# Small heads' outputs computed with the values stationary, on four 32-column strips, and transposed back

## The chip, the cores and the metric

One Trainium2 chip, one of its cores. The metric is the device time of one execution in microseconds (us). TensorE is called PE here, VectorE DVE, ScalarE ACT, GpSimd POOL, SyncE SP.

## What is computed

Thirty-two sequences of 128 tokens with 128 features pass through four blocks. All data is float32.

- L0: a transformer decoder layer (self attention, cross attention, feed forward; 16 heads of 64), on the whole path of each group.
- L1: attention with 16 heads of 8 features. With `q = relu(x Wq + bq)`, `k`, `v` alike, it is `softmax(q k' / sqrt(8)) v + x`.
- L2: an encoder and decoder layer with linear attention.
- L3: layer norms, attention with 8 heads of 16 features, then a linear recurrence over the 128 tokens and a projection.

The change touches one product in L1 and L3, the softmax weights times the values:

```
attn = jax.nn.softmax(score, axis=-1)
a = jnp.einsum('bhqk,bhkd->bhqd', attn, vh)      # d = 8 (L1) or 16 (L3)
```

The kernel leaves the weights unnormalised (exp(score - max)), carries a column of ones beside each head's values, so that one product gives both the sum over the values and the sum of the weights, and divides afterwards.

## The kernel before

The sequences are worked on in 8 groups of 4 (`G = 4`). There are two streams of work, written as generators and interleaved step by step in the same way on every engine. The **main** stream computes L0 of group g, in the order of the table `MAIN_ORDER` (160 steps). The **side** stream computes L1, L2 and L3 of group g-1, in 85 steps; `SIDE_AT` (L84) says before the end of which main step each side step is taken. So there is a first pass with main alone, seven passes with both (pass 1 to pass 7 below), and then group 8's L1 to L3 with nothing of L0 left: there `last(i)` runs beside `ahead(i)`, the part that does not wait for it. The recurrence and the output end the program. Every engine executes its own list strictly in order and waits on semaphores; so an instruction that waits holds everything behind it on its engine.

The small attentions are `attention_small` (side) and `attention_last` (last group). The unit of work is four heads of one sequence: 4 units per sequence in L1 (`per = 4`), 2 in L3 (`per = 2`), and two units make a pair: 8 pairs in L1, 4 in L3, 12 per pass. A pair's steps:

1. `scores` (L942, in the last group L1128): two products, 512 columns each, into banks 5 and 6 of PSUM.
2. DVE takes the maxima (`maxes`, L1688), ACT the exponentials (`exps`, L1441, 8 instructions of 128 columns in the side stream, the `s_probs` rows).
3. PE transposes the weights, 8 transposes of 128x128 (L969, last: L1135), ACT and DVE copy them to `s_probsT`.
4. `outputs` (L955, last: L1149): per head one product with the transposed weights (128x128) as the stationary operand and the head's values as the moving one, which has 9 columns in L1 and 17 in L3. It is issued behind the scores of the next pair. The result has the tokens on the partitions:

```
for h in range(4):
    at = (q * 4 + h) * d1
    last = mm(bank(SIDE, (tag, "o", b))[:, at:at + d1], s_probsT[:, n, h * 128:h * 128 + 128],
              value[:, b, q * 4 + h, :], start=True, stop=True)
```

5. Once per sequence DVE divides (`divide`, L1809 and L1811; in L1 also an addition, L1816) straight out of bank 7.

A float32 product appears in the trace as two LDWEIGHTS (PEld) and two MATMUL records, so 8 products are "x16"; a transpose is one record of each. Of the main stream these lines are spoken of: L810 (projections, 512 columns), L858 (scores of the large heads, 64 rows of the array each), L868 (transposes), L882 (outputs of the large heads, two heads side by side on two halves of the array's columns), L854 (masks), the ACT copies at L1435 and the exponentials in `probs`. `keep_busy` (L800) issues bf16 products whose result nobody reads.

The arrays of the streams' fills (`side_fills`, `last_fills`) list which bank each item is put in and which engine empties it; the counts that semaphores are waited for come from them.

Of the kernel before, what the change touches and what calls it, by code (L numbers as in the profile page):

```python
# [31 lines left out]
G = 4  # L32
# [27 lines left out]
def main_items(name):  # L60
# [11 lines left out]
    if name == "mk":  # L72
# [70 lines left out]
def side_fills():  # L143
# [3 lines left out]
    def attention(tag):  # L147
        per = SMALL[tag][0] // 2
        for j in range(PAIRS[tag] + 1):
            if j < PAIRS[tag]:  # L150
                order.extend(((tag, "s", 2 * j + n), 5 + n, "A") for n in range(2))
            if j and j % per == 0:
                order.append(((tag, "o", j // per - 1), 7, "D"))
            if j < PAIRS[tag]:
                order.extend(((tag, "t", 2 * j + n), 5 + n, "AD"[n]) for n in range(2))

# [30 lines left out]
def last_fills():  # L187
# [8 lines left out]
    def attention(tag):  # L196
# [8 lines left out]
        for j in range(pairs):  # L205
            order.extend(((tag, "t", 2 * j + n), (5, 6, 0, 1)[2 * (j % 2) + n], "AD"[n]) for n in range(2))
            scalar.extend([(tag, "s", 2 * j + 2)] if j + 1 < pairs else [])
            scalar.append((tag, "t", 2 * j))
            scalar.extend([(tag, "s", 2 * j + 3)] if j + 1 < pairs else [])
            if j and j % per == 0:  # L210
                order.append(((tag, "o", j // per - 1), 7, "D"))
            if j + 2 < pairs:
                scores(j + 2)
        order.append(((tag, "o", G - 1), 7, "D"))
# [105 lines left out]
def build_program(nc, I, out):  # L320
    with ExitStack() as ctx:
# [76 lines left out]
        l1v = sb("l1v", [128, G, H1, D1 + 1])  # L398
        l2v = sb("l2v", [128, G, 129])
        l3v = sb("l3v", [128, G, H3, D3 + 1])  # L400
# [40 lines left out]
        l3b_last = queries[:, 1, :]  # L441
        x2_all = sb("x2_all", [128, T, B])
# [144 lines left out]
        def _(pool):  # L587
# [28 lines left out]

            link(P.memset(l1v[:, :, :, D1:D1 + 1], 1.0))
# [31 lines left out]
            def side(i):  # L649
# [17 lines left out]
                for _ in range(3 * PAIRS["l1"] + 1):  # L667
# [33 lines left out]
                for _ in range(3 * PAIRS["l3"] + 1):  # L701
# [10 lines left out]
            def last(i):  # L712
# [9 lines left out]
                for _ in range(2 * PAIRS["l1"] + 2):  # L722
# [29 lines left out]
                for _ in range(2 * PAIRS["l3"] + 2):  # L752
# [37 lines left out]
        def _(pe):  # L790
# [139 lines left out]
            def attention_small(i, tag, value):  # L930
# [14 lines left out]
                def outputs(j):  # L945
                    b = 2 * j // per
                    for n in range(2):
# [12 lines left out]
                for j in range(PAIRS[tag]):  # L960
# [5 lines left out]
                    for n in range(2):  # L966
# [18 lines left out]
            def side(i):  # L985
# [12 lines left out]
                yield from attention_small(i, "l1", l1v)  # L998
# [71 lines left out]
                yield from attention_small(i, "l3", l3v)  # L1070
# [47 lines left out]
            def attention_last(i, tag, value, spread_keys):  # L1118
# [20 lines left out]
                def outputs(j):  # L1139
                    b = 2 * j // per  # L1140
                    for n in range(2):
# [3 lines left out]
                        if q == 0:  # L1145
                            hold(i, LAST, (tag, "o", b))
                        for h in range(4):
                            at = (q * 4 + h) * d1
                            last = mm(bank(LAST, (tag, "o", b))[:, at:at + d1],  # L1149
                                      last_probsT[j % 2][:, n, h * 128:h * 128 + 128],  # L1150
                                      value[:, b, q * 4 + h, :], start=True, stop=True)
# [6 lines left out]
                for j in range(PAIRS[tag]):  # L1158
                    keep_busy(4, 4)
                    turns(j)  # L1160
                    yield
                    keep_busy(0, 4)
# [4 lines left out]
                    yield  # L1167
                outputs(PAIRS[tag] - 1)
                yield
# [969 lines left out]
```

## Time and profile before

| what | value |
|---|---|
| median of 3 runs | 2230.75 us (2226.66 to 2233.94) |
| the profiled execution's own time | 2236.29 us |
| its span, first to last instruction | 2234.6 us |
| mean granted clock of TensorE | 0.961 of 2.4 GHz |
| PE busy | 1989.1 us, 89% |
| DVE, ACT, POOL busy | 60%, 49%, 11% |
| chain that ended last | PE 59%, DVE 21%, ACT 15%, issue 4% |

The profile's page gives busy shares, the chain of work that ended last (followed back from the last instruction, at each step to what released it) and groups of instructions. The timeline, the chain in order of time, and windows (busy time and granted clock of a stretch) come from the trace of the same execution. The granted clock is a share of full speed: 0.50 is the lower of its two levels, 1.2 GHz, and 1.00 the upper, 2.4 GHz.

### The profile page before, as it was taken

To read this page: it belongs to the slowest core of one execution; us is meant where nothing else is said; L and a number is where in the kernel's file an instruction comes from. 1 tells how busy PE (TensorE), PEld (TensorE's weight loads), DVE (VectorE), ACT (ScalarE), POOL (GpSimd) and SP (SyncE) were. 2 spreads that over 40 slices of the span, in tenths; PEclk is the share of its full clock that TensorE was granted. 3 is DMA by queue.
4 is the path that set the end of the run, shared out by engine and by line. 5 is a ranking of instruction groups with operands and counts; after the bars stand their busy time and mean duration, and the time that the engine had idled before them with its cause. 6 is when DMAs were issued, how large, how long until landed. Compare 5 with 4: busy or idle time off the path is not lost.

```text
span 2234.6 us, 35672 instructions
## 1 busy us (share of the span) xinstructions
PE 1989.1 (89%) x13350; PEld 1347.7 (60%) x13457; DVE 1332.3 (60%) x3612; ACT 1093.0 (49%) x3794; POOL 238.2 (11%) x261
## 2 busy tenths in 40 slices
PE   6877998899889998899889998899889998888799
PEld 3555665657656665656656675656656675656455
DVE  4443667566675667566675667666675657654410
ACT  4452745557362735546363645547363745533222
POOL 0001011010112011010111001010212001010100
PEclk9998999999999999999999999999999999998999
DMA  6000000000000000000000000000000000000001
GB/s 186 1 1 16 1 1 1 1 16 1 1 1 16 1 1 1 1 16 1 1 1 16 1 1 1 1 16 1 1 1 5 1 1 1 1 1 1 1 11 28
DMA packets 25137, 20.13 MB, mean 9 GB/s; under 512 B 2243, under 2 KB 22790, under 8 KB 24966
## 3 DMA queue, kind: packets, MB, share of 16 engines
q1 hardware_dynamic: 24966, 17.83, 2.8%
q8 instruction: 109, 1.79, 0.3%
q14 instruction: 62, 0.51, 0.1%
HBM read 15.73 MB, written 2.10 MB: 8 GB/s over the span
## 4 chain that ended last, share of the span: by engine, by line
PE 59%; DVE 21%; ACT 15%; issue 4%; POOL 1%; SPq 1%; DMA 0%; POOLq 0%; DVEq 0%; ACTq 0%
PE ps L810 13%; PE ps L818 10%; ACT probs L1441 7%; PE ps L858 6%; PE ps L955 5%; ACT s_probs L1441 4%; PE ps L882 3%; DVE neg_max L1688 3%; PE ps L969 3%; PE ps L806 3%; PE ps L800 2%; PE ps L868 2%; PE ps L942 2%; PE ps L854 2%; PE ps L1389 2%
## 5 line engine op out<-in xcount | busy, mean ns | idle before, releaser
L1441 ACT ACTIVATE probs<-ps,neg_max 128x128 f32<-128x128 f32 x1024 | 360.3, 378 | 248.2 <-DVE neg_max L1688 247.2
L1688 DVE TENSOR_REDUCE neg_max<-ps 128x4 f32<-128x512 f32 x256 | 164.6, 685 | 126.7 <-PE ps L858 126.6
L1441 ACT ACTIVATION_READ_ACCUMULATOR probs<-ps,neg_max 128x1 f32 x1024 | 221.8, 217 | 0.0
L632 POOL TENSOR_TENSOR rstd<-var_eps,minus_half 128x4 f32<-128x4 f32 x88 | 94.4, 1073 | 1125.9 <-DVE var_eps L1701 1125.9
L1695 DVE BATCH_NORM_STATS2 stats<-ps 128x6 f32<-128x128 f32 x352 | 78.2, 284 | 215.2 <-PE ps L818 207.0
L1441 ACT ACTIVATE s_probs<-ps,s_max 128x128 f32<-128x128 f32 x672 | 185.5, 425 | 22.5 <-DVE s_max L1688 22.5
L1435 ACT ACTIVATE probsT<-ps 128x512 f32<-128x512 f32 x262 | 160.2, 631 | 72.6 <-PE ps L868 70.5
L1730 DVE TENSOR_TENSOR probs<-probs,inv 128x512 f32<-128x512 f32 x256 | 180.3, 704 | 8.8
L868 PE MATMUL ps<-ident,probs 128*128 128x128 f32 x1024 | 159.2, 284 | 15.0 <-ACT queries L1435 6.9
L858 PEld LDWEIGHTS ps<-keys,queries 64*128 64x128 f32 x2048 | 130.6, 196 | 57.7 <-issue 57.7
L868 PEld LDWEIGHTS ps<-ident,probs 128*128 128x128 f32 x1024 | 119.1, 146 | 68.0 <-issue 28.2
L858 PE MATMUL ps<-keys,queries 64*128 64x128 f32 x2048 | 155.8, 294 | 0.0
L810 PE MATMUL ps<-xT_a,w_qkv_sa 128*128 128x512 f32 x256 | 145.3, 662 | 5.8 <-ACT xT_a L1435 2.9
L882 PE MATMUL ps<-probsT,values 128*64 128x128 f32 x2048 | 145.9, 286 | 5.0 <-ACT probsT L1435 5.0
L882 PEld LDWEIGHTS ps<-probsT,values 128*64 128x64 f32 x2048 | 114.3, 141 | 40.2 <-issue 33.3
L955 PEld LDWEIGHTS ps<-l1v,s_probsT 128*128 128x128 f32 x896 | 104.8, 192 | 39.4 <-issue 37.2
L1688 DVE TENSOR_REDUCE s_max<-ps 128x4 f32<-128x512 f32 x168 | 107.9, 684 | 29.8 <-PE ps L942 29.8
L800 PE MATMUL ps<-ident_h 128*128 128x512 bf16 (+1 forms) x452 | 121.4, 377 | 0.0
L969 PE MATMUL ps<-ident,s_probs 128*128 128x128 f32 x672 | 106.6, 300 | 15.7 <-ACT s_probs L1441 14.6
L1464 ACT ACTIVATE keys<-ps,col_all 128x512 f32<-128x512 f32 x64 | 44.4, 693 | 153.8 <-PE ps L810 153.8
L1826 DVE COPY s_probsT<-ps 128x512 f32<-128x512 f32 x84 | 58.0, 691 | 102.2 <-PE ps L969 102.1
L969 PEld LDWEIGHTS ps<-ident,s_probs 128*128 128x128 f32 x672 | 86.9, 156 | 52.9 <-ACT s_probs L1441 33.0
(294 smaller groups left out, 3584.5 us busy)
## 6 DMA issues: line engine op xcount, KB each, us to landing
x_in<-in_x SPq DMA_DIRECT2D x8, 256.0 KB, 4.2
c_in<-in_ctx SPq DMA_DIRECT2D x8, 256.0 KB, 4.8
skip_in<-in_mask_BxS_ik SPq DMA_DIRECT2D x8, 256.0 KB, 4.0
out<-headsT SPq DMA_DIRECT2D x28, 64.0 KB, 1.8
valid_in<-in_mask_BxS_bf SPq DMA_DIRECT2D x8, 64.0 KB, 2.9
w_qkv_sa<-in_L_xattn_sa_wq SPq DMA_DIRECT2D x1, 512.0 KB
w_qkv_sa<-in_L_xattn_sa_wk SPq DMA_DIRECT2D x1, 512.0 KB
w_qkv_sa<-in_L_xattn_sa_wv SPq DMA_DIRECT2D x1, 512.0 KB
```

Source lines behind the costliest of these rows:

```text
L800: mm(ps[:, unused, 0:width], ident_h[:, :], ident_h[:, :].unsqueeze(1).broadcast_to([128, width // 128, 128]), start=True, stop=True)
L810: mm(bank(st, name)[0:lhs.shape[-1], :], lhs, rhs, start=True, stop=True).then_inc(filled[st], 1)
L818: last = mm(dst, l, r, start=(n == 0), stop=(n == len(todo) - 1))
L858: last = mm(bank(MAIN, (tag, "s", u + h))[:, b * T:b * T + T], queries[rows_of, c % 2, b * T:b * T + T], keys[rows_of, c % 2, b * T:b * T ...
L868: last = nc.tensor.transpose(bank(MAIN, item)[:, h * 128:h * 128 + 128], probs[:, u % 4, h * 128:h * 128 + 128], ident[:, :])
L882: last = mm(bank(MAIN, item)[64 * h:64 * h + 64, b * T:b * T + T], values[:, c // 4, b, at:at + 64], probsT[:, u % PT, b * T:b * T + T], s ...
L955: last = mm(bank(SIDE, (tag, "o", b))[:, at:at + d1], s_probsT[:, n, h * 128:h * 128 + 128], value[:, b, q * 4 + h, :], start=True, stop=True)
L969: last = nc.tensor.transpose(bank(SIDE, (tag, "t", 2 * j + n))[:, h * 128:h * 128 + 128], s_probs[:, n, h * 128:h * 128 + 128], ident[:, :])
L1435: A(dst, view(s) if view else s, fn, **kw).then_inc(emptied[st, "A"], 1)
L1441: last = A(dst[:, u % dst.shape[1], h * 128:h * 128 + 128], bank(st, (tag, "s", u))[:, h * 128:h * 128 + 128], ACT.Exp, bias=src_max[:, u ...
L1688: V.tensor_reduce(dst[:, u % 2, :], bank(st, (tag, "s", u)).rearrange("p (h k) -> p h k", h=4), AX.X, ALU.max, negate=True).then_inc(max_r ...
L1730: V.tensor_tensor(p, p, inv[:, u % 4, :].unsqueeze(2).broadcast_to([128, G, T]), ALU.mult).then_inc(scaled, 1)
```

## The change

The product of step 4 is turned round. The stationary operand is now a tile of 32 columns of the values that begins at the head's first column (its 9 or 17 columns, and after them columns of the next heads, which are computed and not used), and the moving operand is the transposed weights, 128 columns. The four heads of a unit write to the partitions 0, 32, 64 and 96 on, so to four strips of the array's columns. The result, item `w`, has features on the partitions; ACT copies it to SBUF (512 columns in L1, 256 in L3, once per sequence), and PE transposes it back (`heads_back`, 4 or 2 transposes) into item `o` in bank 7, which DVE divides as before, now with heads 32 columns apart. `heads_back` stands a step later than the copy, the division one more; a side step is added to each attention (at main steps 69 and 150), so the side stream has 87. In the last group the `keep_busy(4, 4)` ahead of each pair's transposes is dropped. The values get 32 columns of zeros behind them, set once.

```
+            def head_products(st, tag, u, turned_probs):
+                per, d1 = SMALL[tag]
+                b, q = u // per, u % per
+                for h in range(4):
+                    at = ((b * per + q) * 4 + h) * d1
+                    last = mm(bank(st, (tag, "w", b))[32 * h:32 * h + 32, q * T:q * T + T], value_row[tag][:, at:at + 32],
+                              turned_probs[:, h * T:h * T + T], start=True, stop=True)
+                return last
+            def heads_back(i, st, tag, b):
+                wait_emptied(pe, i, st, (tag, "w", b))
+                for q in range(SMALL[tag][0]):
+                    last = nc.tensor.transpose(bank(st, (tag, "o", b))[:, q * T:q * T + T], outs_at[st][:, q, :], ident[:, :])
+                last.then_inc(filled[st], 1)
...
             def attention_small(i, tag):
                         if q == 0 and b:
                             wait_emptied(pe, i, SIDE, (tag, "o", b - 1))
-                        for h in range(4):
-                            at = (q * 4 + h) * d1
-                            last = mm(bank(SIDE, (tag, "o", b))[:, at:at + d1], s_probsT[:, n, h * 128:h * 128 + 128],
-                                      value[:, b, q * 4 + h, :], start=True, stop=True)
+                        last = head_products(SIDE, tag, u, s_probsT[:, n, :])
...
                         last.then_inc(filled[SIDE], 1)
+                    if j and 2 * j % per == 0:
+                        heads_back(i, SIDE, tag, 2 * j // per - 1)
                     yield
                 outputs(PAIRS[tag] - 1)
+                yield
+                heads_back(i, SIDE, tag, G - 1)
...
             def attention_last(i, tag, spread_keys):
                 for j in range(PAIRS[tag]):
-                    keep_busy(4, 4)
                     turns(j)
-                    yield
-                    keep_busy(0, 4)
+                    if j >= 2 and 2 * (j - 1) % per == 0:
+                        heads_back(i, LAST, tag, 2 * (j - 1) // per - 1)
+                    yield
...
             def attention_small(i, tag, before):      # ACT
                         exps(i, SIDE, tag, before, 2 * j + n, s_max, s_probs)
                     yield
+                    if j and 2 * j % per == 0:
+                        take(i, SIDE, (tag, "w", 2 * j // per - 1), outs_at[SIDE][:, 0:per, :], ACT.Copy, width=per * T,
+                             view=lambda s: s.rearrange("p (q n) -> p q n", n=T))
                     yield
...
             def attention_small(i, tag):              # DVE
                 for j in range(PAIRS[tag]):
+                    if j >= 2 and 2 * (j - 1) % per == 0:
+                        divide(2 * (j - 1) // per - 1)
                     for n in range(2):
                         maxes(i, SIDE, tag, 2 * j + n, s_max)
-                    if j and 2 * j % per == 0:
-                        divide(2 * j // per - 1)
```

**Where instructions move.** PE in pass 1, from the scores of the fifth pair of L1 to the next masks, before (L942 scores, L955 outputs, L969 and L868 transposes, L854 masks):

```order
L942 MATMUL ps<-kx,qT 128x512 x2
L955 MATMUL ps<-l1v,s_probsT 128x9 x8
L810 MATMUL ps<-xT_a,w_qkv_sa 128x512
L868 MATMUL ps<-ident,probs 128x128 x4
L882 MATMUL ps<-probsT,values 64x128 x8
L868 MATMUL ps<-ident,probs 128x128 x4
L969 MATMUL ps<-ident,s_probs 128x128 x8
L868 MATMUL ps<-ident,probs 128x128 x4
L854 MATMUL ps<-mask_sa,ident_h 128x512 x2
```

And with the change (the same places are L974, L951, L998 and L883, L869; L959 is `heads_back`):

```order
L951 MATMUL ps<-s_probsT,l1v 32x128 x8
L825 MATMUL ps<-xT_a,w_qkv_sa 128x512
L883 MATMUL ps<-ident,probs 128x128 x4
L897 MATMUL ps<-probsT,values 64x128 x8
L883 MATMUL ps<-ident,probs 128x128 x4
L998 MATMUL ps<-ident,s_probs 128x128 x8
L959 MATMUL ps<-ident,l2v 128x128 x4
L883 MATMUL ps<-ident,probs 128x128 x4
L869 MATMUL ps<-mask_sa,ident_h 128x512 x2
L873 MATMUL ps<-keys,queries 128x128 x8
```

The outputs stand where they stood; four transposes that read ACT's copy (`l2v`) stand behind the transposes of the weights, ahead of the main stream's.

ACT at the same pair, from the side stream's exponentials on, before and after:

```order
L1441 ACTIVATE s_probs<-ps,s_max 128x128 x8
L1435 ACTIVATE probsT<-ps 128x512
L1435 ACTIVATE headsT<-ps 128x512
L1435 ACTIVATE probsT<-ps 128x512
L1435 ACTIVATE s_probsT<-ps 128x512
```

```order
L1474 ACTIVATE s_probs<-ps,s_max 128x128 x8
L1468 ACTIVATE probsT<-ps 128x512
L1468 ACTIVATE headsT<-ps 128x512
L1468 ACTIVATE probsT<-ps 128x512
L1468 ACTIVATE l2v<-ps 128x4x128
L1468 ACTIVATE s_probsT<-ps 128x512
```

The copy of `w` to `l2v` stands behind three copies of the main stream.

PE at the end of the last group's second attention, before (L1149 outputs, L1135 transposes, L800 `keep_busy`) and after (L951 outputs, L959 transposes back, L1168 transposes, L815 `keep_busy`):

```order
L1149 MATMUL ps<-l3v,probsT 128x17 x8
L800 MATMUL ps<-ident_h 128x512 x2
L1135 MATMUL ps<-ident,probs 128x128 x8
L1149 MATMUL ps<-l3v,s_probsT 128x17 x8
L1149 MATMUL ps<-l3v,probsT 128x17 x8
L806 MATMUL ps<-ident,tok 128x128 x4
```

```order
L951 MATMUL ps<-probsT,l3v 32x128 x8
L1168 MATMUL ps<-ident,probs 128x128 x8
L959 MATMUL ps<-ident,probsT 128x128 x2
L951 MATMUL ps<-s_probsT,l3v 32x128 x8
L959 MATMUL ps<-ident,probsT 128x128 x2
L951 MATMUL ps<-probsT,l3v 32x128 x8
L959 MATMUL ps<-ident,probsT 128x128 x2
L821 MATMUL ps<-ident,tok 128x128 x4
```

Each of the last sequences' outputs is now followed by transposes back that wait for ACT, and the next outputs wait for the division.

## Rows read from the trace of the kernel before

**Rows 1.** Page: engines' busy time, and the clock granted in 40 slices.
```profile
PE 1989.1 (89%) x13350; PEld 1347.7 (60%) x13457; DVE 1332.3 (60%) x3612; ACT 1093.0 (49%) x3794; POOL 238.2 (11%) x261
...
PEclk9998999999999999999999999999999999998999
```

**Rows 2.** Page: the chain that ended last, by line.
```profile
PE ps L810 13%; PE ps L818 10%; ACT probs L1441 7%; PE ps L858 6%; PE ps L955 5%; ACT s_probs L1441 4%; PE ps L882 3%; DVE neg_max L1688 3%; PE ps L969 3%; PE ps L806 3%; PE ps L800 2%; PE ps L868 2%; PE ps L942 2%; PE ps L854 2%; PE ps L1389 2%
```

**Rows 3.** Windows, passes 1 to 7: start:end, length, busy per engine, PEclk, DMA.
```profile
221.35:471.19 249.84, 227.63 (x1581) 156.97 (x1595) 164.69 (x448) 132.99 (x459) 29.91 (x32) 0.98 0.02 5
471.19:720.09 248.90, 226.18 (x1581) 155.86 (x1595) 165.03 (x448) 132.67 (x459) 29.90 (x32) 0.99 0.02 4
720.09:974.96 254.87, 232.57 (x1581) 160.30 (x1595) 164.90 (x448) 133.49 (x459) 29.88 (x32) 0.96 0.02 4
974.96:1228.54 253.58, 231.28 (x1581) 158.18 (x1595) 164.88 (x448) 132.96 (x459) 29.88 (x32) 0.97 0.02 4
1228.54:1481.88 253.34, 231.04 (x1581) 158.99 (x1595) 164.91 (x448) 133.50 (x459) 29.90 (x32) 0.97 0.02 4
1481.88:1730.52 248.64, 226.19 (x1581) 155.79 (x1595) 164.91 (x448) 132.74 (x459) 29.90 (x32) 0.99 0.01 2
1730.52:1976.60 246.08, 223.35 (x1555) 154.05 (x1569) 159.51 (x437) 129.72 (x454) 25.42 (x28) 0.97 0.00 1
```

**Rows 4.** Windows of the same kind, low-clock stretches: the first, a middle, the last.
```profile
239.50:242.50 3.00, 3.00 (x11) 2.08 (x10) 0.00 (x0) 2.63 (x8) 0.00 (x0) 0.50 0.00 0
659.00:662.50 3.50, 3.28 (x22) 2.44 (x23) 1.00 (x2) 1.53 (x4) 0.00 (x0) 0.52 0.02 5
1809.50:1813.00 3.50, 3.50 (x14) 2.11 (x10) 1.38 (x2) 1.67 (x7) 0.00 (x0) 0.52 0.00 0
```

**Rows 5.** Timeline of PE around 758: start, us, engine, line.
```profile
755.47 1.95 PE L955 MATMUL ps<-l1v,s_probsT 128*128 128x9 f32 x16
757.28 2.94 PE L810 MATMUL ps<-xT_a,w_qkv_sa 128*128 128x512 f32 x4
```

**Rows 6.** Chain by time, pass 2 from 490: start, us, what.
```profile
493.40 1.06 PE ps L942 x4
494.46 1.88 PE ps L955 x16
496.34 1.82 PE ps L810 x4
498.16 1.02 PE ps L882 x16
499.18 1.02 PE ps L868 x8
500.21 0.87 PE ps L969 x8
```

**Rows 7.** Chain by time, pass 2 from 522.
```profile
522.55 0.68 DVE neg_max L1688
...
523.26 2.90 ACT probs L1441 x16
...
526.74 2.07 ACT s_probs L1441 x8
528.81 0.49 ACT probsT L1435
```

**Rows 8.** Timeline of all engines, pass 2 around 520.
```profile
519.51 1.04 PE L969 MATMUL ps<-ident,s_probs 128*128 128x128 f32 x8
...
520.67 0.73 ACT L1435 ACTIVATE s_probsT<-ps 128x512 f32<-128x512 f32 x1
```

**Rows 9.** Windows: the first attention of the last group.
```profile
1981.50:2050.15 68.65, 58.69 (x346) 44.50 (x346) 34.99 (x101) 29.02 (x85) 4.64 (x4) 0.84 0.00 1
```

**Rows 10.** Timeline of PE: end of the last group's second attention.
```profile
2120.53 1.86 PE L1149 MATMUL ps<-l3v,s_probsT 128*128 128x17 f32 x16
2123.11 3.26 PE L1149 MATMUL ps<-l3v,probsT 128*128 128x17 f32 x16 [0.72 <-DVE tok L1946]
```

More of the change, by code:

```diff
@@ L152, in attention @@
             if j and j % per == 0:
-                order.append(((tag, "o", j // per - 1), 7, "D"))
+                order.append(((tag, "w", j // per - 1), 7, "A"))
             if j < PAIRS[tag]:
                 order.extend(((tag, "t", 2 * j + n), 5 + n, "AD"[n]) for n in range(2))
+            if j and j % per == 0:
+                order.append(((tag, "o", j // per - 1), 7, "D"))
     order += [(("l1", "q"), 5, "D"), (("l1", "k"), 6, "A"), (("l1", "v"), 7, "D")]
@@ L206, in attention @@
             order.extend(((tag, "t", 2 * j + n), (5, 6, 0, 1)[2 * (j % 2) + n], "AD"[n]) for n in range(2))
+            if j >= 2 and (j - 1) % per == 0:
+                order.append(((tag, "o", (j - 1) // per - 1), 7, "D"))
             scalar.extend([(tag, "s", 2 * j + 2)] if j + 1 < pairs else [])
@@ L210, in attention @@
             if j and j % per == 0:
-                order.append(((tag, "o", j // per - 1), 7, "D"))
+                order.append(((tag, "w", j // per - 1), 7, "A"))
+                scalar.append((tag, "w", j // per - 1))
             if j + 2 < pairs:
                 scores(j + 2)
+        if (pairs - 1) % per == 0:
+            order.append(((tag, "o", G - 2), 7, "D"))
+        order.append(((tag, "w", G - 1), 7, "A"))
+        scalar.append((tag, "w", G - 1))
         order.append(((tag, "o", G - 1), 7, "D"))
@@ L666, in side @@
                     yield
-                for _ in range(3 * PAIRS["l1"] + 1):
+                for _ in range(3 * PAIRS["l1"] + 2):
                     yield
@@ L700, in side @@
                 yield
-                for _ in range(3 * PAIRS["l3"] + 1):
+                for _ in range(3 * PAIRS["l3"] + 2):
                     yield
@@ L721, in last @@
                 yield
-                for _ in range(2 * PAIRS["l1"] + 2):
+                for _ in range(2 * PAIRS["l1"] + 3):
                     yield
@@ L751, in last @@
                 yield
-                for _ in range(2 * PAIRS["l3"] + 2):
+                for _ in range(2 * PAIRS["l3"] + 3):
                     yield
@@ L1145, in outputs @@
                         if q == 0:
[L1146 to L1151, printed above, removed]
+                            hold(i, LAST, (tag, "w", b))
+                        last = head_products(LAST, tag, u, last_probsT[j % 2][:, n, :])
                     if q == per - 1:
@@ L1481, in attention_small @@
                     yield
+                take(i, SIDE, (tag, "w", G - 1), outs_at[SIDE][:, 0:per, :], ACT.Copy, width=per * T,
+                             view=lambda s: s.rearrange("p (q n) -> p q n", n=T))
+                yield
                 yield
@@ L1557, in attention_last @@
                     yield
+                    if j and 2 * j % per == 0:
+                        take(i, LAST, (tag, "w", 2 * j // per - 1), outs_at[LAST][:, 0:per, :], ACT.Copy, width=per * T,
+                             view=lambda s: s.rearrange("p (q n) -> p q n", n=T))
                     yield
+                take(i, LAST, (tag, "w", G - 1), outs_at[LAST][:, 0:per, :], ACT.Copy, width=per * T,
+                             view=lambda s: s.rearrange("p (q n) -> p q n", n=T))
+                yield
                 yield
@@ L1827, in attention_small @@
                     yield
+                if 2 * (PAIRS[tag] - 1) % per == 0:
+                    divide(G - 2)
+                yield
                 divide(G - 1)
@@ L1960, in attention_last @@
                     yield
-                    if j and 2 * j % per == 0:
-                        divide(2 * j // per - 1)
+                    if j >= 2 and 2 * (j - 1) % per == 0:
+                        divide(2 * (j - 1) // per - 1)
                     if j + 2 < PAIRS[tag]:
@@ L1965, in attention_last @@
                     yield
+                if 2 * (PAIRS[tag] - 1) % per == 0:
+                    divide(G - 2)
+                yield
                 divide(G - 1)
```

31 lines of the change are left out of this document (21 added, 10 removed), and 6 rows, old and new, of the table SIDE_AT.

## The prediction

> **What bounds the kernel now.** Read the page's busy times first: PE works 89% of the span, the next engine far less, and the clock granted to PE is near full in nearly every slice [rows 1]. PE leads, but the chain that ended last gives the outputs in question (L955) only 5% of the span [rows 2], about 103 us, although their 84 groups in passes 1 to 7 take 84 x 1.88 [rows 6] = 158 us. So part of them is hidden behind something already. Two further views show behind what, and at what clock.
>
> The chain in order of time, read in pass 2 round by round (a round goes from one L858 of the main stream to the next), has rounds of two kinds. In the one at 490 PE is back to back, scores, outputs, projections, transposes [rows 6]. In the one at 522 the chain leaves PE: DVE's maximum, 0.68, ACT's main exponentials, 2.90, its side exponentials, 2.07, a copy [rows 7]; the transposes L969 need their end. This ladder is 5.65 us long behind every L858, and PE must have that much work between L858 and L969 or stand.
>
> The windows by pass give the clock: lengths of 248.6 to 254.9 us with the same instructions [rows 3]. I looked for stretches at the lower level in windows of half a microsecond: 27 in passes 1 to 7, by pass 3, 2, 6, 5, 5, 2 and 4, each 3 to 3.5 us long; the first, one of the middle and the last are [rows 4]. The two passes with 2 take 248.8, the two with 5 take 253.5, the one with 6 takes 254.9: 1.5 us for each stretch. What PE did before the fall: in 21 of the 27 an L955 group was still running or had ended within the 1.5 us before, as at 758 [rows 5], where the projections behind it take 2.94 against 1.82 at the upper level [rows 6]. In the other 6 PE had stood waiting, mostly for ACT ahead of L969, as at 659 [rows 4]. An L955 group keeps PE busy in the profile for 1.9 us, but streams 9 or 17 columns per record; most of it is loading weights.
>
> **The change, part by part.**
>
> *Outputs, shorter on PE.* 8 products of 9 columns: 1.88 [rows 6], 0.116 per record, which is weight loading. Now 16 records of 128 columns on four strips. L882 does 16 such records on two halves in 1.02 [rows 6], What leaving the tiled form costs, L942 shows: two 512-column products side by side take 1.06, one alone (half of L810's 1.82 for two) 0.91, so 0.15 more. That leaves L882 0.87 of streaming; I take half of it for four strips, 0.43, and the 0.15, rounded to 0.60 together. Bounds: 1.02 if four strips gain nothing over two, 1.88 if they don't overlap at all. Saving 1.28 per pair, 0.86 at the one bound, nothing at the other. The leaving is new: L955 was in the same form as what follows.
>
> The Trainium skill ("TensorEngine Tiling (Array Packing)", Key Properties) states that a change of tiling mode drains TensorE, which speaks against this change. The 0.15 agrees in kind and is in the sum; were a drain twice as dear here, 84 x 0.15 = 13 us of PE time would come on top, at most 13 us in the sum.
>
> *Transposes back.* 16 in L1 and 8 in L3 per pass. A transpose is 0.87 / 8 = 0.11 [rows 6]: 0.44 for four, 0.22 for two, 2.6 per pass.
>
> *Copies on ACT.* Per pass 4 of 512 columns at 0.49 [rows 7] and 4 of 256; these are between the 0.26 of 128 columns (2.07 / 8) and 0.49, I take 0.37. 3.4 per pass, of which only those on the ladder count.
>
> *What of this is on the path, in an undisturbed pass.* The gain of a round is at most PE's work between L858 and L969 less the ladder. In the round at 490: 1.06 + 1.88 + 1.82 + 1.02 + 1.02 = 6.80 against 5.65, so the first 1.15 of the saving counts, and 0.44 of transposes goes off: +0.7. In the next the work is 1.06 (a projection) + 1.06 + 1.88 + 1.82 = 5.82: +0.2. In the round that ends at 520 it is 5.9: +0.3, but here the new transposes stand behind L969, which ends at 520.5, and wait for a copy that ACT issues behind three others of the main stream, where now s_probsT begins at 520.67 [rows 8]; with 0.49 it ends at 521.2, and 0.44 of transposes follow: the masks start 1.15 later. That round loses 1.15. The next two are ladders already [rows 7]: nothing gained, and in the second the copy stands right behind the exponentials and ahead of the copies that L858 waits for: -0.5. The seventh, with a main projection between, gives +0.3. At the end of L1 outputs, copy and transposes follow one another: 0.60 + 0.49 + 0.44 and two hand-overs of some 0.1 against 1.88, +0.1. In L3 the copy costs the second round 0.4, the last one gives 0.35, and the end, outputs, copy, transposes in place of outputs alone, 0.3. Sum, rounded: -0.1 us a pass. With 0.86 saved per pair in place of 1.28 it is -1.2. The gain of 1.28 x 12 = 15 us of PE time a pass is nearly all hidden by the ladder; what is late next is ACT. The later division on DVE stands ahead of the side maxima, which wait for the scores anyway; where the next outputs wait for it, they wait inside the 1.28 that they have saved.
>
> *The clock.* Wherever PE now streams 9 columns for 1.9 us it will stream 128 for 0.5 and then either go on with full products or stand for up to 1.3. That is never less work in the array than now. I expect three quarters of the 21 falls of this kind to go: 16 x 1.5 = 24 us.
>
> *The last group.* Its L1 attention takes 68.7 us with PE busy 58.7 at a mean clock of 0.84 [rows 9]. Off it come 8 x 1.28 and eight pairs of `keep_busy` products (an estimate: a pair as half of a float32 product of 512 columns, 0.45): 13.8; on it go 16 transposes, 1.8. Half of the rest counts, as DVE and ACT ladders lie beside it: 6. In L3 four pairs come to wait for a copy and a division each; but at the end 1.86 + 0.72 + 3.26 [rows 10] becomes twice outputs 0.60, copy 0.37, transposes 0.22 and division with its hand-overs 0.72: 3.8, so 2 off. Together 8, between 2 on and 16 off.
>
> Elsewhere nothing moves: no DMA is touched; two memsets at the start lie under the first weights' load. The side stream's own steps behind each attention come one step later.
>
> **Sum.** 7 x 0.1 on, 24 off, 8 off: 31 us off the profiled execution's 2236.3, which is 5.5 above the median of the runs shown; off the median, 2230.75 - 31 = **2200 us**.
>
> **Rivals.**
>
> *PE's time counts after all.* If ACT's ladder is looser than pass 2 shows, the chain's own share decides: 103 us x 1.28 / 1.88 = 70 off, 8 x 2.6 = 21 on, and 24 off for the clock: 2158. For it: L955 stands on the chain at all. Against: the ladder of 5.65 behind each L858.
>
> *The low stretches stay.* PE waits more, and the falls ahead of L969 show that waiting too is followed by one. A pass then stays as it is and the last group gives 6: 2225. A rule of the Trainium skill points this way ("TensorE: Matmul & The Clock Gate", Part 4): transposes don't count as busy for the clock, and this change adds some. That the round at 490, half of it transposes, is at full clock says little either way.
>
> *Slower: the copies of w on ACT become the path.* If each transpose back waits as the one at 520 does, a pass gets 4 x 1.15 in L1 and 4 x 0.7 in L3 (a copy, its transposes, a hand-over) = 7.4 longer and keeps 1.5 from the open rounds: 7 x 5.9 = 41 on; with half of the clock's gain and the last group's, 16 off: 2256. It decides from the point where ACT's queue at the copy is later than PE's last weight transpose; in pass 2 that holds for one of eight.
>
> *It does not do what it says:* the four strips run one after another. The outputs cost 1.88 still, transposes and copies come on top, about 3 us a pass, but the columns stream and the clock stays up: 21 on, 24 off, 2228.
>
> **Chances.** Forecast 0.55, PE's time 0.10, low stretches stay 0.13, copies 0.12, no overlap 0.10. A difference of 0.3%, 6.7 us, is what these runs can tell. Faster: 0.55 + 0.10 and a third of the two in the middle, 0.73; slower: 0.12 and a little, 0.14; same 0.13. The range reaches from the forecast with all 21 falls gone, the last group at its best and 1 us more in each pass (32 + 16 + 7 off: 2176) to passes that lose 1.2 each with no fall gone and the last group at its worst (8 + 2 on: 2240); beyond lie the first rival and most of the third.
>
> **What would show it.** The w products, 16 records in about 0.45 us; PE less busy in passes, with waits for ACT's copy ahead of the transposes back, most in the round of the fifth pair of L1; ACT's ladder unchanged; 10 or so low stretches in passes 1 to 7, and passes near 249 us. I am wrong if passes with few low stretches differ from 248.8 by over 2 us, or if their number stays at 20 and more.

## The result, and the profile after

The changed kernel takes 2262.4 us (median of 4 runs, 2258.7 to 2268.0), the kernel before 2228.7 beside it: ratio 1.0149, 95% interval 1.0126 to 1.0172, so 1.5% slower, 33 us. The profiled execution took 2259.8, its span is 2258.1, its mean granted clock 0.968 (0.961 before). The two profiled executions, from which everything below is read, lie 23.5 us apart and not 33: the profiled one of before is slower than that kernel's median.

The page of the changed kernel, engines and the chain that ended last [rows 1, 2]; L825 is L810 of before, L833 L818, L873 L858, L1474 L1441, L1735 L1688:

```profile
PE 1913.7 (85%) x13625; PEld 1214.3 (54%) x13625; DVE 1327.7 (59%) x3612; ACT 1115.2 (49%) x3858; POOL 238.4 (11%) x263
...
PE 49%; DVE 24%; ACT 21%; issue 4%; POOL 1%; SPq 1%; DMA 0%; POOLq 0%; DVEq 0%; ACTq 0%
PE ps L825 10%; PE ps L833 10%; ACT probs L1474 10%; ACT s_probs L1474 6%; PE ps L873 6%; DVE neg_max L1735 5%; PE ps L821 3%; PE ps L815 3%; PE ps L869 3%; PE ps L897 2%; DVE stats L1742 2%; PE ps L1422 2%; DVE tok L1755 2%; PE ps L883 2%; PE ps L998 2%
```

PE works 75 us less and the kernel is longer: PE's share of the chain fell from 59% to 49%, ACT's and DVE's rose from 36% to 45%.

Windows by pass and, as the last row, of the last group [rows 3]; columns as there:

```profile
219.65:476.77 257.12, 222.20 (x1618) 142.71 (x1619) 164.18 (x448) 135.88 (x467) 29.91 (x32) 0.97 0.02 4
476.77:732.10 255.33, 220.43 (x1619) 141.35 (x1619) 164.32 (x448) 135.74 (x467) 29.91 (x32) 0.98 0.02 4
732.10:987.90 255.80, 220.90 (x1619) 141.77 (x1619) 164.38 (x448) 135.83 (x467) 29.89 (x32) 0.98 0.02 4
987.90:1246.43 258.53, 223.74 (x1619) 143.40 (x1619) 164.39 (x448) 135.81 (x467) 29.88 (x32) 0.97 0.02 4
1246.43:1500.58 254.15, 219.24 (x1619) 140.49 (x1619) 164.30 (x448) 135.81 (x467) 29.90 (x32) 0.99 0.02 4
1500.58:1756.04 255.46, 220.55 (x1619) 141.44 (x1619) 164.40 (x448) 135.83 (x467) 29.91 (x32) 0.98 0.01 2
1756.04:2006.07 250.03, 214.58 (x1593) 138.15 (x1593) 158.99 (x437) 132.03 (x462) 25.42 (x28) 0.98 0.00 1
2006.07:2258.10 252.03, 202.87 (x1218) 117.77 (x1218) 83.34 (x241) 78.18 (x272) 17.22 (x14) 0.93 0.04 9
```

The seven passes are 31.2 us longer (1786.4 against 1755.2), the stretch before them 1.7 shorter, the last group 6.0 shorter (252.0 against 2234.6 - 1976.6 = 258.0). The 6.0 is not firm: the same instructions of the last group took 258.2 and 259.5 in two kernels below (e2, e6), at a mean granted clock of 0.89 in place of 0.93.

The products themselves came out as costed. Timeline of PE, pass 2:

```profile
499.96 0.64 PE L951 MATMUL ps<-s_probsT,l1v 128*32 128x128 f32 x16
500.54 1.12 PE L825 MATMUL ps<-w_qkv_sa,xT_a 128*128 128x512 f32 x2
```

16 records in 0.58 to the next start; 0.60 was in the sum. The waits of PE in the seven passes say what took the gain away (engine, line, what it waited for: us in total, times, longest; the first line is of before, the others of the changed kernel, where L998 is L969 of before):

```profile
PE ps L969 <- ACT s_probs L1441: 14.6, 27, 1.3
...
PE ps L998 <- ACT s_probs L1474: 48.4, 91, 1.3
PE ps L951 <- DVE x1T L1863: 22.3, 21, 2.3
PE ps L821 <- DVE tok L1755: 18.6, 21, 1.6
PE ps L959 <- ACT l2v L1468: 17.6, 21, 1.3
PE ps L1057 <- DVE s_probs L1915: 16.9, 14, 1.3
PE ps L951 <- DVE tok L1858: 14.9, 7, 2.1
```

Three kinds of wait are new or longer; the others of this list are in the kernel before with the same sums. The transposes of the weights (L998) wait 34 us more for ACT's exponentials: time that PE saved on the outputs and spends waiting for the ladder. The `w` products (L951) wait 37.2 us for **divisions** (x1T in L1, tok in L3), the transposes back (L959) 17.6 for ACT's copy. The dearest single place is the end of L3. Timeline of PE and DVE there, pass 2:

```profile
696.80 0.39 PE L833 MATMUL ps<-ident,main_residual 128*128 128x128 f32 x2
697.23 0.89 DVE L1742 BATCH_NORM_STATS2 stats<-ps 128x6 f32<-128x128 f32 x4 [7.57 <-PE ps L833]
...
698.88 0.29 DVE L1858 TENSOR_TENSOR tok<-ps,s_inv 128x128 f32<-128x128 f32 x1
699.31 0.65 PE L951 MATMUL ps<-s_probsT,l3v 128*32 128x128 f32 x16 [2.13 <-DVE tok L1858]
700.46 0.44 PE L959 MATMUL ps<-ident,l2v 128*128 128x128 f32 x2 [0.50 <-ACT l2v L1468]
...
702.07 3.52 PE L815 MATMUL ps<-ident_h 128*128 128x512 bf16 x8
```

The third sequence's transposes back ended at 689.1, but its division stands in DVE's list behind the main stream's layer norm, whose statistics wait 7.57 us for PE's last L833. PE stands 2.13, and behind it the clock is at its lower level: the same eight bf16 products (`keep_busy`, L815) take 3.52 here and took 1.89 in the kernel before (in six passes of seven):

```profile
691.69 1.89 PE L800 MATMUL ps<-ident_h 128*128 128x512 bf16 x8
```

Windows of three such stretches of the changed kernel, [rows 4] for before:

```profile
552.00:555.00 3.00, 2.64 (x32) 2.23 (x32) 1.41 (x3) 2.16 (x8) 0.00 (x0) 0.50 0.00 0
650.50:654.00 3.50, 2.88 (x15) 1.98 (x16) 2.94 (x7) 0.00 (x0) 0.00 (x0) 0.53 0.00 0
702.00:705.50 3.50, 3.50 (x11) 1.38 (x10) 0.74 (x3) 0.60 (x1) 0.00 (x0) 0.52 0.00 0
```

There are 22 of them in the passes where before had 27, but now 20 at the same three places: L1's last pair (552, in all seven passes), ahead of L3 (650.5, in six) and L3's end (702, in all seven). Each begins during a wait of PE or within 3 us of its end. The wait ahead of L3, 1.6 for normalised tokens, is one that the kernel before has too; the other two are new. L1's last pair, PE and DVE:

```profile
549.51 0.59 PE L974 MATMUL ps<-kx,qT 32*128 32x512 f32 x2
...
550.70 0.69 DVE L1777 TENSOR_TENSOR probs<-probs,inv 128x512 f32<-128x512 f32 x1
...
551.92 0.29 DVE L1863 TENSOR_TENSOR x1T<-tok,x_bias 128x128 f32<-128x128 f32 x1
...
552.36 1.08 PE L951 MATMUL ps<-s_probsT,l1v 128*32 128x128 f32 x16 [2.25 <-DVE x1T L1863]
```

The division is ahead of the side maxima, as the prediction says, but behind the main stream's products of weights and sums (L1777). The fifth pair of L1 has the third new wait, for ACT's copy; no fall of the clock follows this one in any pass:

```profile
525.35 0.72 ACT L1468 ACTIVATE probsT<-ps 128x512 f32<-128x512 f32 x1
...
525.83 0.73 ACT L1468 ACTIVATE l2v<-ps 128x512 f32<-128x512 f32 x1
...
526.61 0.66 PE L959 MATMUL ps<-ident,l2v 128*128 128x128 f32 x4 [1.29 <-ACT l2v L1468]
```

### The profile page after: what moved, and what is told of

Same layout as the page of the kernel before. It is cut to its first block, busy times and chain, and to the rows that moved or that the text cites. A ratio compares the mean times of both kernels' runs of the same rounds, so it can differ in the third digit from the quotient of the medians.

```text
span 2258.1 us, 36181 instructions
## 1 busy us (share of the span) xinstructions
PE 1913.7 (85%) x13625; PEld 1214.3 (54%) x13625; DVE 1327.7 (59%) x3612; ACT 1115.2 (49%) x3858; POOL 238.4 (11%) x263
## 4 chain that ended last, share of the span: by engine, by line
PE 49%; DVE 24%; ACT 21%; issue 4%; POOL 1%; SPq 1%; DMA 0%; POOLq 0%; DVEq 0%; ACTq 0%
PE ps L825 10%; PE ps L833 10%; ACT probs L1474 10%; ACT s_probs L1474 6%; PE ps L873 6%; DVE neg_max L1735 5%; PE ps L821 3%; PE ps L815 3%; PE ps L869 3%; PE ps L897 2%; DVE stats L1742 2%; PE ps L1422 2%; DVE tok L1755 2%; PE ps L883 2%; PE ps L998 2%
## 5 line engine op out<-in xcount | busy, mean ns | idle before, releaser
L1474 ACT ACTIVATE probs<-ps,neg_max 128x128 f32<-128x128 f32 x1024 | 360.3, 378 | 250.1 <-DVE neg_max L1735 249.1
L1735 DVE TENSOR_REDUCE neg_max<-ps 128x4 f32<-128x512 f32 x256 | 164.7, 685 | 157.8 <-PE ps L873 157.8
L1474 ACT ACTIVATION_READ_ACCUMULATOR probs<-ps,neg_max 128x1 f32 x1024 | 221.9, 217 | 0.0
L1468 ACT ACTIVATE probsT<-ps 128x512 f32<-128x512 f32 (+1 forms) x270 | 165.3, 635 | 67.1 <-PE ps L883 56.9
L1474 ACT ACTIVATE s_probs<-ps,s_max 128x128 f32<-128x128 f32 x672 | 185.5, 426 | 24.9 <-DVE s_max L1735 24.9
L1777 DVE TENSOR_TENSOR probs<-probs,inv 128x512 f32<-128x512 f32 x256 | 180.3, 704 | 8.8
L883 PE MATMUL ps<-ident,probs 128*128 128x128 f32 x1024 | 157.1, 281 | 17.6 <-ACT queries L1468 6.9
L873 PEld LDWEIGHTS ps<-keys,queries 64*128 64x128 f32 x2048 | 131.0, 196 | 58.0 <-issue 58.0
L873 PE MATMUL ps<-keys,queries 64*128 64x128 f32 x2048 | 156.0, 294 | 0.0
L883 PEld LDWEIGHTS ps<-ident,probs 128*128 128x128 f32 x1024 | 115.6, 142 | 71.5 <-issue 32.6
L998 PE MATMUL ps<-ident,s_probs 128*128 128x128 f32 x672 | 105.9, 285 | 50.1 <-ACT s_probs L1474 48.4
L825 PE MATMUL ps<-xT_a,w_qkv_sa 128*128 128x512 f32 x256 | 138.6, 634 | 8.0 <-ACT xT_a L1468 2.9
L998 PEld LDWEIGHTS ps<-ident,s_probs 128*128 128x128 f32 x672 | 73.4, 142 | 99.6 <-ACT s_probs L1474 90.8
L815 PE MATMUL ps<-ident_h 128*128 128x512 bf16 (+1 forms) x428 | 121.4, 397 | 0.0
L1735 DVE TENSOR_REDUCE s_max<-ps 128x4 f32<-128x512 f32 x168 | 107.8, 683 | 18.8 <-PE ps L974 18.7
L821 PE MATMUL ps<-ident,tok 128*128 128x128 f32 x336 | 56.4, 292 | 47.7 <-DVE tok L1755 26.4
```

What stands on the lines that cost most here:

```text
L815: mm(ps[:, unused, 0:width], ident_h[:, :], ident_h[:, :].unsqueeze(1).broadcast_to([128, width // 128, 128]), start=True, stop=True)
L821: last = nc.tensor.transpose(bank(st, name)[:, b * 128:b * 128 + 128], src(b), ident[:, :])
L825: mm(bank(st, name)[0:lhs.shape[-1], :], lhs, rhs, start=True, stop=True).then_inc(filled[st], 1)
L873: last = mm(bank(MAIN, (tag, "s", u + h))[:, b * T:b * T + T], queries[rows_of, c % 2, b * T:b * T + T], keys[rows_of, c % 2, b * T:b * T ...
L883: last = nc.tensor.transpose(bank(MAIN, item)[:, h * 128:h * 128 + 128], probs[:, u % 4, h * 128:h * 128 + 128], ident[:, :])
L998: last = nc.tensor.transpose(bank(SIDE, (tag, "t", 2 * j + n))[:, h * 128:h * 128 + 128], s_probs[:, n, h * 128:h * 128 + 128], ident[:, :])
```

## The experiments

The kernel before was run again beside each group of experiments, and its median lay between 2228.3 and 2232.2 us. A difference between times that were not measured side by side is therefore good to some 4 us; the ratios are to the kernel before as it ran beside them.

**A ruler.** The main stream's maxima (`neg_max`) come 32 times in a pass and in the same order in every kernel, so the interval from the start of one to the start of the next, as the median over passes 2 to 6, shows each place apart. Below, differences against experiment e4, whose passes have six falls, the fewest of the kernels in the table; the stretches that differ by over 0.1, worked out from the timelines:

```
stretch behind maximum      e4      before   changed   e3      e5      e6
 3  (L1, third pair)        7.77    +1.08    +0.02    +0.01   +0.02   +0.02
 5                          9.46     0       -0.17    -0.16   -0.17   -0.17
 7                          9.65     0       -0.25    -0.25   -0.25   -0.25
 9  (L1, fifth pair)        8.17     0       +1.57    +1.57   +0.16   +1.57
13                          8.64     0       +0.31    +0.31   +0.31   +0.31
15  (L1, last pair, end)   48.43    +1.30    +2.85    +0.26   +0.25   +2.70
25  (ahead of L3)          13.05     0       +1.39    +1.35   +0.01   +1.37
29                          7.34    +1.40    +0.01    +0.01   +0.02   +0.01
31  (L3 end, next pass)    61.94    -0.05    +3.78    -0.10   -0.16   -0.10
pass                      246.1    249.8    255.7    249.2   246.3   251.7
```

A fall alone shows as 1.3 to 1.5 (25, 29), a wait alone as 1.57 (9), and the two places with a new wait for a division and a fall as 2.85 and 3.78 (15, 31).

**e4, 64 moving columns in the old form.** Is it the streamed columns that the clock's falls follow?

```
-  last = mm(bank(SIDE, (tag, "o", b))[:, at:at + d1], s_probsT[:, n, h * 128:h * 128 + 128],
-            value[:, b, q * 4 + h, :], start=True, stop=True)
+  row = b * per * 4 * d1 + at
+  last = mm(bank(SIDE, (tag, "o", b))[:, at:at + 64], s_probsT[:, n, h * 128:h * 128 + 128],
+            value_row[tag][:, row:row + 64], start=True, stop=True)     # the last group likewise
```

> The kernel before with its own products, whose moving operand is 64 columns wide in place of 9 or 17 (the columns behind a head's own are overwritten by the next heads' products or never read). A record takes the same time if the weight load of 0.116 us sets it (64 columns stream in about 0.114, a fourth of a 512-column product's 0.91 for two records over two). Theory of the prediction (falls of the clock follow the products because they stream only 9 columns): the 21 low stretches of this kind in passes 1 to 7 go, at 1.5 us each 31 us off, 2198 us. Rival: the falls follow PE's waits, or come by the weight loads as such; then the number of low stretches stays at 20 and more and the time at 2229 us. A third case: 64 columns are dearer than the weight load; then the group takes over 2 us and the time is above 2229.

Measured: 2202.1 us, ratio 0.9864 (0.9842 to 0.9886). Low stretches in the passes: 6. The group takes what it took:

```profile
489.61 2.00 PE L961 MATMUL ps<-l1v,s_probsT 128*128 128x64 f32 x16
491.44 1.08 PE L815 MATMUL ps<-w_qkv_sa,xT_a 128*128 128x512 f32 x2
```

1.83 to the next start against 1.81 for 9 columns [rows 5]. Windows of passes 2 to 4 and of the last group:

```profile
466.43:712.51 246.08, 224.51 (x1595) 153.80 (x1595) 164.91 (x448) 132.42 (x459) 29.86 (x32) 1.00 0.02 5
712.51:960.14 247.63, 226.07 (x1595) 154.80 (x1595) 165.16 (x448) 132.49 (x459) 29.84 (x32) 0.99 0.02 5
960.14:1207.63 247.49, 226.06 (x1595) 154.82 (x1595) 164.97 (x448) 132.49 (x459) 29.85 (x32) 0.99 0.02 5
...
1946.38:2199.30 252.92, 218.04 (x1218) 135.49 (x1218) 83.97 (x241) 74.68 (x264) 17.21 (x14) 0.93 0.04 9
```

By [rows 6] a record of 512 columns takes 1.82 / 4 = 0.455, so one of 64 about 0.06 (an estimate); the 0.114 that was expected is what 128 columns would take. 27 - 6 = 21 stretches at 1.5 us are 31; 30 were measured. So the prediction's reading, that most falls follow the products of few columns, is shown, and all that the change could win in the passes was to be had with no new instruction but two memsets. A pass with no fall takes 246.1, with one 247.6.

**e3, the divisions a step earlier.**

```
                 for j in range(PAIRS[tag]):          # DVE, side
-                    if j >= 2 and 2 * (j - 1) % per == 0:
-                        divide(2 * (j - 1) // per - 1)
                     for n in range(2):
                         maxes(i, SIDE, tag, 2 * j + n, s_max)
                     yield
                     yield
                     take(i, SIDE, (tag, "t", 2 * j + 1), lambda x: V.tensor_copy(s_probsT[:, 1, :], x))
+                    if j and 2 * j % per == 0:
+                        divide(2 * j // per - 1)
                     yield
-                if 2 * (PAIRS[tag] - 1) % per == 0:
-                    divide(G - 2)
                 yield
```

> In the changed kernel's side stream the division of a sequence stands a step earlier on DVE: directly behind the copy to s_probsT whose transposes are followed by the transposes back, in place of ahead of the next maxima (L1) or behind the main stream's layer norm (L3's end). Theory: the wait is the loss. The wait at L3's end goes (2.1 us, and the keep_busy behind it at the upper clock again, 1.6 us less), and so do the waits of w for the division in L1 (2.3 us before the last pair, 0.8 and 0.2 before). That is 5.5 to 6 us of each of 7 passes: 2262 - 40 = 2222 us, and the falls of the clock at 552 and 702 us and their like in the other passes go. Rival: DVE now stands waiting for the transposes back, which wait for ACT's copy, and holds up the main stream's work on DVE by as much; then 2250 us or more.

Measured: 2218.2 us, ratio 0.9935 (0.9915 to 0.9955). That is 44 us below the changed kernel (48 by the ratios) by an edit that moves the two or three short instructions of a division; 7 low stretches in the passes. The rival, that DVE's own waits cost as much, is out. Windows of passes 2 to 4:

```profile
471.37:720.59 249.22, 218.15 (x1618) 139.67 (x1619) 164.48 (x448) 135.61 (x467) 29.90 (x32) 0.99 0.02 5
720.59:969.79 249.20, 218.12 (x1618) 139.63 (x1619) 164.56 (x448) 135.71 (x467) 29.88 (x32) 0.99 0.02 5
969.79:1218.99 249.20, 218.12 (x1619) 139.61 (x1619) 164.59 (x448) 135.72 (x467) 29.89 (x32) 0.99 0.02 4
```

Passes 2 to 6 each take 249.2, with one fall, always at the same place, ahead of L3 (643, 892.5, 1141.5 us and on), behind waits of PE for normalised tokens of 1.6 and 0.6.

**e6, only the division at L3's end moved.** The same edit for `j == PAIRS[tag] - 1` in L3 alone.

> The changed kernel with one division moved: that of the third sequence in L3, from behind the main stream's layer norm to behind the last copy of transposed weights. Theory: this place costs 3.8 us of each pass, 2.1 of waiting and 1.6 for the products of keep_busy behind it at the lower clock: 7 x 3.8 = 27 us off 2262, so 2235 us; the other 17 us up to the 2218 of the kernel with all divisions earlier are those of L1. Rival: the fall of the clock only moves to another place; then 15 off, 2247 us.

Measured: 2240.3 us (10 runs), ratio 1.0041 (1.0019 to 1.0063): 22 off (24 by the ratios), between the two, 27 and 15. PE and DVE at the place:

```profile
694.08 0.39 PE L833 MATMUL ps<-ident,main_residual 128*128 128x128 f32 x2
694.40 0.64 PE L951 MATMUL ps<-s_probsT,l3v 128*32 128x128 f32 x16
694.50 0.89 DVE L1742 BATCH_NORM_STATS2 stats<-ps 128x6 f32<-128x128 f32 x4 [7.13 <-PE ps L833]
...
697.10 1.89 PE L815 MATMUL ps<-ident_h 128*128 128x512 bf16 x8
```

No wait, and L815 at 1.89. By the table stretch 31 gives back 3.9 a pass, 27 in all, and by the windows the seven passes 23; the rest went into other falls (18 remain, where 22 less the 7 of this place would be 15) and, in the profiled execution, into a last group of 259.5 at a clock of 0.89.

**e5, ACT's copy ahead of the main stream's copies,** on top of e3.

```
                     for n in range(2):               # ACT, side
                         exps(i, SIDE, tag, before, 2 * j + n, s_max, s_probs)
-                    yield
                     if j and 2 * j % per == 0:
                         take(i, SIDE, (tag, "w", 2 * j // per - 1), ...)
+                    yield
                     yield
```

> On top of the earlier division (2218 us): in the side stream ACT copies w directly behind the side's exponentials, ahead of the main stream's copies, in place of behind them. Theory: the transposes back of L1's fifth pair wait 1.29 us for this copy behind three others; the wait goes, 1.3 x 7 = 9 us off, and where the copy now stands ahead of the copy that the large heads' outputs wait for, at most 0.5 us comes on in two or three rounds of a pass: net 0 to 9 off, 2212 us. Rival: PE waits there for something behind the copy as well (the copy of the transposed weights or the normalised weights), and nothing is gained: 2218 or more.

Measured: 2208.8 us (2208.3 to 2210.8), ratio 0.9900 (0.9873 to 0.9926). At the fifth pair the transposes back no longer wait:

```profile
520.07 0.70 ACT L1468 ACTIVATE l2v<-ps 128x512 f32<-128x512 f32 x1
520.34 0.66 PE L998 MATMUL ps<-ident,s_probs 128*128 128x128 f32 x4 [0.38 <-ACT s_probs L1474]
...
520.83 0.65 PE L959 MATMUL ps<-ident,l2v 128*128 128x128 f32 x4
```

Stretch 9 gives back 1.41, and no stretch lost by it. A pass with no fall takes 246.3 in this profiled execution; in e9 below, with the same side stream, it takes 246.06, as in e4.

**The last group, five kernels.** e1 undoes it there alone, e2 does it there alone, e8 puts `keep_busy(4, 4)` back ahead of `turns(j)` on e3, e9 moves the last group's divisions a step forward on e5, e10 is e5 with the old last group. The edit of e9:

```
                 for j in range(PAIRS[tag]):          # DVE, last group
                     take(i, LAST, (tag, "t", 2 * j + 1), ...)
-                    yield
                     if j >= 2 and 2 * (j - 1) % per == 0:
                         divide(2 * (j - 1) // per - 1)
+                    yield
```

> The last group's two attentions are put back to the form of before (products of 9 and 17 columns, keep_busy, no copy, no transposes back); the side stream keeps the change. Read from the two traces, the changed kernel lost 31.2 us in passes 1 to 7 and gained 6.0 us in the last group. Theory: the two parts do not act on each other, so this kernel takes 2262 + 6 = 2268 us. Rival: the last group gained only because of how the passes left it (state of the clock); then it takes 2262 us as the changed kernel does.

Measured: 2271.0 us (2263.9 to 2274.0), ratio 1.0170 (1.0146 to 1.0193): above the changed kernel by 9 us, by 5 if one goes by the ratios. In the profiled execution its passes, which are the changed kernel's, take 8 us more than there, so not all of it is the last group's.

> The side stream's attentions are put back to the form of before (its list keeps the two added empty steps); the last group keeps the change. Theory: 2229 - 6 = 2223 us, the passes as in the kernel before. Rival: 2229 or more, if the gain of the last group was a matter of the clock alone, or if the added steps themselves cost.

Measured: 2228.8 us against 2232.2, ratio 0.9987 (0.9972 to 1.0002): 3 us off, not clear of noise.

> The kernel with the earlier divisions (2218 us), and keep_busy(4, 4) put back ahead of each pair's transposes in the last group. Theory: PE waits for ACT's exponentials at that place for longer than the 0.9 us that two such products take, so they cost nothing, and the clock is if anything higher: 2214 to 2218 us. Rival, the step of the prediction: half of each counts, 12 x 0.9 / 2 = 5 us on, 2223 us.

Measured: 2216.2 us, ratio 0.9925 (0.9899 to 0.9952); e3 without them has 0.9935. No cost is to be seen: at the first of the places PE's wait for the exponentials behind them is 1.37 where it was 1.91 without.

> The side stream of the kernel with earlier divisions and copies (2208.8 us), the last group in the form of before. Theory: the turned products gain 3 us in the last group (the kernel with them there alone: 2228.8 against 2232.2), so this one takes 2212 us. Rival, the prediction's term: 8 us, so 2217.

Measured: 2206.8 us, ratio 0.9907 (0.9882 to 0.9931), e5's own time within 2 us and under both that were expected. So with the late divisions the gain of the turned products in the last group is nothing by e10, 3 us by e2 and 5 to 9 by e1; the runs do not settle it further.

> On top of the kernel with earlier divisions and copies in the side stream (2208.8 us): in the last group too, the division stands a step earlier, behind the copy of the transposed weights. In that kernel the last group's w waits 5.0 us once, 8.8 in all, for a division that stands behind a layer norm of the work beside it. Theory: the same fault as in the side stream; 5 to 8 us off, 2202 us. Rival: PE's wait only goes over to the normalised tokens that the product two places further waits for anyway; then 2207 or more.

Measured: 2195.7 us, ratio 0.9858 (0.9834 to 0.9881). The largest wait, in e5 and then the same products in e9:

```profile
1994.54 1.08 PE L951 MATMUL ps<-s_probsT,l1v 128*32 128x128 f32 x16 [5.03 <-DVE x1T L2000]
```

```profile
1981.70 0.29 DVE L2000 TENSOR_TENSOR x1T<-tok,x_bias 128x128 f32<-128x128 f32 x1
1982.66 0.64 PE L951 MATMUL ps<-s_probsT,l1v 128*32 128x128 f32 x16
1982.76 0.89 DVE L1742 BATCH_NORM_STATS2 stats<-ps 128x6 f32<-128x128 f32 x4 [0.77 <-PE ps L833]
```

The same fault as in the side stream: the division stood behind a layer norm of the work that runs beside it. 13 us came off where 5 to 8 were expected. In the two profiled executions, 14.1 apart, the last group takes 251.5 against 255.3 and the passes 1727.6 against 1729.3; the other 8.7 lie ahead of pass 1 (215.9 against 224.5), where the two programs are the same and the mean granted clock was 0.96 in e9 and 0.92 in e5. So in these two executions the edit is worth about 4 us in the last group, and most of the rest is the clock ahead of pass 1; what split the other executions is not known.

**Combinations of the two forms.** Old form with 64 columns in the side stream; turned products in the last group, with late (e7) and early (e11) divisions.

> The side stream computes its outputs in the form of before with a moving operand of 64 columns (2202 us with the same in the last group); the last group has the turned products. Theory: the turned products gain in the last group what they gained there alone, about 3 us: 2199 us. Rival: what the last group gained was the clock, which the 64 columns give back as well (its last group took 252.9 us, the changed kernel's 252.0); then 2202 or a little more.

Measured: 2203.7 us, ratio 0.9876 (0.9845 to 0.9906): no gain over e4, as the rival has it.

> The side stream in the form of before with 64 moving columns, the last group with the turned products and its divisions a step earlier; with the later divisions it took 2203.7 us. Theory: 5 to 8 us off, 2197 us, below the 2202.1 of 64 columns in both. Rival: as for the kernel before this one in the list; then 2203.

Measured: 2198.5 us, ratio 0.9867 (0.9845 to 0.9888): 5 us under e7, as expected, though the two intervals overlap.

e4, e9 and e11 can't be told apart. Two versions beat the kernel before by 1.4%, and the changed one by more: the old products with 64 columns (e4), and the turned ones with divisions and copies early enough (e9). e4 is the smaller edit.

## Why the prediction was wrong

Forecast 2200, range 2176 to 2240, measured 2262.4. Point by point:

- **Cost of the turned products: right.** 0.58 per group against 0.60; four strips overlap, so the fourth rival (one after another, 1.88) is out. ACT's copy takes 0.47 to the next one (525.83 to 526.30) against 0.49, the four transposes 0.50 (526.61 to 527.11) against 0.44. By [rows 6] a record of 128 columns streams in 0.455 / 4 = 0.114, so four rounds of four strips in 0.455 (an estimate), which leaves 0.13 of the 0.58 for leaving the tiled form; 0.15 was in the sum. The Trainium skill's drain at a change of tiling mode ("TensorEngine Tiling (Array Packing)", Key Properties) can't have been dearer than that here.
- **The undisturbed pass, -0.1: right only with other places for division and copy.** PE's saved time is hidden by the ladder: e4 with 224.5 us of PE work in a pass takes 246.08, e9 with 216.4 takes 246.06. For the kernel as written it was wrong by far: the passes are 9.6 us longer than e4's by the table, falls included.
- **The failed step: "The later division on DVE stands ahead of the side maxima, which wait for the scores anyway; where the next outputs wait for it, they wait inside the 1.28 that they have saved."** The sum has nothing for this wait. The DVE list was not read through. In L1's last pair the main stream's L1777 stands ahead of the division, and at L3's end its whole layer norm. The waits are 2.25 and 2.13, not under 1.28. e3 shows the price, wait and falls together: 44 us, of which L3's end is 22 (e6).
- **Fifth pair, 1.15 later: right in its place and cause,** 1.57 in size; e5 takes it away.
- **The clock, 24 us off: right as a mechanism** (e4, 30 us; 27 stretches to 6), **and lost in this kernel,** because the two new waits of over 2 us come with a fall in all seven passes, though the one of 1.29 at the fifth pair comes with none. 22 stretches remain, and only with the waits for divisions gone are there 7 (e3). Such a wait must be charged the fall too: 3.8 a pass at L3's end is 2.1 of wait and 1.6 of clock. The round at 490 is a quarter transposes (1.89 of 7.67 us in [rows 6]), not half as the prediction has it. The Trainium skill's rule on transposes ("TensorE: Matmul & The Clock Gate", Part 4) didn't decide: e5 has all of the new transposes and 7 stretches, e4 none of them and 6.
- **The last group, 8 us off: nothing by e10, 3 by e2, 5 to 9 by e1,** so the term was probably too large. It took keep_busy as cost, and e8 shows none. And its division had the same fault.
- **The rivals.** "Low stretches stay" was half of the truth (22 of 27), "copies of w on ACT become the path" had the sign and nearly the time, 2256, but not the cause: the copies account for the fifth pair's 1.4 us a pass, 10 in all, the divisions for 44.

What stays open: why the fall ahead of L3 comes in each of passes 2 to 6 of e3 and in few of e4's and e5's, with the same waits ahead of it. The stretch ahead of pass 1 took between 215.9 and 224.5 us in kernels that don't differ there; it goes with the granted clock (0.96 and 0.92 at the two ends), and why the clock differed there is open.

## What to carry to other kernels

When a result gets one stage more between its product and its consumer (here copy, transposes back, division), read every engine's list at each place where the stage lands, to the end of the loop: a short instruction behind another stream's layer norm holds the next product for as long as that stream needs. Price a new wait of PE with the slow stretch that may follow it; here those of over 2 us had one every time. And before turning a product round for the clock, widen its moving operand up to what the weight load hides: here it gave as much as any version reached, within the noise.

## What the runs showed of the hardware that was not expected

- 8 float32 products of 64 moving columns take 1.83 us, those of 9 take 1.81, and the first are followed by far fewer falls of the granted clock: 6 against 27 in seven passes, 30 us.
- Four strips of 32 columns ran their 128-column products together: 16 records in 0.58 us, where 16 on two halves take 1.02 [rows 6].
- Where the same wait of PE is followed by a fall in every pass, the passes repeat to 0.04 us (249.18 to 249.22, passes 2 to 6 of e3). e5's executions spread over 2.5 us (2208.3 to 2210.8), those of before, run beside it, over 25 (2219.5 to 2244.6); but e7, with 8 low stretches to e5's 7, spreads over 11, so few falls alone don't explain it.
- In the changed kernel the waits of PE of 2.25 and 2.13 us came with a fall of the granted clock in all seven passes, the one of 1.29 at the fifth pair in none.
- The same instructions of the last group took 252.0 us at a mean granted clock of 0.93 and 259.5 at 0.89: a stretch's difference between two kernels means little until its clock is compared.
